# Loading an adjacency pair from two DMA queues: lower half on SyncE's, upper half on GpSimd's

## The chip, the cores and the metric

The kernel runs on one core of a Trainium2 chip, and its time is the device time of that core in microseconds. TensorE multiplies, VectorE transposes and does two-input arithmetic, ScalarE evaluates Ln, Exp and Square, GpSimd does a little arithmetic and issues DMAs, and SyncE only issues DMAs. In the profile they are called PE, DVE, ACT, POOL and SP. The 16 DMA engines are shared. A DMA issued by SP shows as q1 (hardware queue) and one issued by POOL as q0 (software queue).

## The reference

Two graph layers over 4096 nodes with 128 features. All matrices are float32, and `adj` is dense with 64 MB.

```python
h = jnp.maximum(_layernorm(x), 0.0)
msg = h @ W0 + B
sens = jnp.exp(-(1.0 / adj - 1.0) ** 2 / (2.0 * 0.5 * 0.5))
x = x + jnp.where(adj < 1.0, sens, 0.0) @ msg            # layer 0

h = jnp.maximum(_layernorm(x), 0.0)
A_hat = adj + jnp.eye(4096)
d = jnp.sum(A_hat, axis=1) ** (-0.5)
x = x + jax.nn.relu((d[:, None] * A_hat * d[None, :]) @ (h @ W1.T))   # layer 1
```

Row block r of layer 1 needs `support` of all column blocks, and `support` of block c needs the finished layer 0 of rows c. So a block (r, c) with c < r can be multiplied at once, and the others are kept for later.

## The kernel before

The matrix is cut in 8 x 8 blocks of 512 x 512 (`G = 8`). A block with its eight row groups is a *unit* u (64 in all, eight per block row, row g holds units 8g to 8g+7), and two units side by side are a *pair* n (32 in all, four per row). A pair is 2 MB and is loaded into `raw[:, n % 2]`: 128 partitions with 16 pieces of 256 floats (1 KB) each. Four DMAs bring it, one per quadrant of 32 partitions (`for q in range(Q)`), 512 KB each. Quadrants 0 and 1 are partitions 0 to 63, the lower half here, and quadrants 2 and 3 are the upper half.

For each unit DVE transposes `raw` into `kept[:, u % 4]` (`turn`, line 648), then takes the entries below the cutoff into `wt[:, u % 6]` (`cut`, line 663). ACT makes the weights from `wt` in four passes (Ln, Exp, Square, Exp: lines 528, 533, 538, 547; for every odd unit of rows 0 to 2 DVE takes over the square, line 669, and ACT's last pass is line 544). PE multiplies `wt` with `msg` into `acc0` (line 377), three units behind DVE (`LAG`). The row sums for layer 1 come from PE in rows 0 to 2 (`sum_tiles`, line 407) and from DVE in rows 3 to 7 (`row_sum`, line 656, once per pair, which reads `raw` too).

A block that layer 1 can use at once is multiplied from `kept` (`mix_once`, line 390). The 35 others are written to memory as 1 MB tiles (`store`, line 291, SP) and loaded again (line 345, POOL) into one of three `late` slots, and at the end into `raw`, for `mix_late` (line 399). Which late tile is multiplied at which unit is written out in the table `JOBS`; 20 late tiles are used inside the loop over units (`IN_TURN`) and 15 behind it (`TAIL`). At the end of each row PE, ACT and DVE pass the finished layer 0 rows to and fro (`copy_x1t` 573, `turn_x1` 430, `make_x1` 745, `log_pows` 577, `copy_hid` 585, `make_support` 774).

Three orders matter here. **SP's queue** is one list: the weights, `x` and pairs 0 and 1, then for each unit u the `store(u)`, if it is kept for later, and after each odd u the four DMAs of pair u // 2 + 2. The load waits until both units of the pair that had the buffer are turned, and from row 3 on until its `row_sum` is done. **POOL's queue** holds four memsets, the identity, 24 `tensor_scalar` for layer 0's first norm (line 330, three groups that wait for DVE's moments) and then the late loads in the order in which they are used. Late load j waits for the multiplication that frees its slot (`late_done`) and for its store (`spilled`). **DVE** waits in `turn` for `raw_loaded` at each even unit. A semaphore counts 16 per DMA.

Of the kernel before, what the change touches and what calls it, by code (L numbers as in the profile page):

```python
# [19 lines left out]
C4 = 4  # L20
Q = 4
B = 32
# [13 lines left out]
def col(u):  # L36

    return ORDER[u // G][u % G]
# [49 lines left out]
    return sum(not squared_by_dve(v) for v in range(u + 1))  # L88

def first_job(u):

    return sum(len(JOBS[v]) for v in JOBS if v < u)
# [10 lines left out]
def slot_before(j):  # L104

    return max((i for i in range(j) if late_slot(i) == late_slot(j)), default=None)

def slot_count(j):
# [4 lines left out]
def build(nc, x, adj, w0, b0, w1, out):  # L114
# [6 lines left out]
    with ctx:  # L121
# [64 lines left out]
        x_loaded = [sem(f"x_loaded{i}") for i in range(C4)]  # L186
        w_loaded = sem("w_loaded")
        raw_loaded = [sem(f"raw_loaded{i}") for i in range(RAW)]
        spilled = [sem(f"spilled{i}") for i in range(KEPT)]
        late_loaded = [sem(f"late_loaded{i}") for i in range(LATE + 2 * RAW)]  # L190
        out_written = [sem(f"out_written{i}") for i in range(2)]
# [80 lines left out]
        @block.sync  # L272
        def _(sp):
            def load(n):
                g = n // C4
                if n >= RAW:
                    if n - RAW >= PE_SUMS * C4:
                        sp.wait_ge(summed, n - RAW + 1 - PE_SUMS * C4)
                    sp.wait_ge(turned, 2 * (n - RAW + 1))
                for q in range(Q):  # L280
                    sp.dma_start(raw[q * B:(q + 1) * B, n % RAW],  # L281
                                 adj_parts[g // 2, g % 2, col(2 * n) // 2, q]).then_inc(raw_loaded[n % RAW], 16)

            def load_x(c):
                for h in range(2):
                    for q in range(Q):
                        sp.dma_start(x1[q * B:(q + 1) * B, c * 8 + h * T:c * 8 + h * T + T],
                                     x_parts[c, h, q]).then_inc(x_loaded[c], 16)

            def store(u):  # L290
                sp.dma_start(spill[u // G, col(u)],
                             kept[:, u % KEPT].rearrange("p k i -> p (k i)")).then_inc(spilled[u % KEPT], 16)

            sp.dma_start(w0_sb[:], w0).then_inc(w_loaded, 16)
            sp.dma_start(w1_sb, w1).then_inc(w_loaded, 16)
            sp.dma_start(b_row, b0.rearrange("(a d) -> a d", a=1)).then_inc(w_loaded, 16)
            load_x(0)
            load(0)
            load_x(1)
            load(1)  # L300
            load_x(2)
            load_x(3)
            for u in range(UNITS):
                if spills(u):
                    sp.wait_ge(turned, u + 1)
                    store(u)
                if u % 2 == 1 and u // 2 + RAW < PAIRS:
                    load(u // 2 + RAW)
            for i, r in enumerate(ENDS):
                sp.wait_ge(out_done, i + 1)  # L310
                for q in range(Q):
                    sp.dma_start(out_parts[r // 2, r % 2, q],
                                 fin[i % 2][q * B:(q + 1) * B]).then_inc(out_written[i % 2], 16)
            for i in range(2):
                sp.wait_ge(out_written[i], 64 * (G // 2))

        @block.gpsimd
        def _(pool):
            nc.gpsimd.memset(ident[:], 0.0).then_inc(ident_zeroed, 1)
            nc.gpsimd.memset(ones_row, 1.0)  # L320
            nc.gpsimd.memset(ones[:], 1.0)
# [9 lines left out]
                                                   ALU.subtract, ALU.max)  # L331
                last.then_inc(h0_done, 1)

            for j, (r, c) in enumerate(LOADED):
                slot = late_slot(j)
                u = r * G + ORDER[r].index(c)
                before = slot_before(j)
                if before is not None:
                    pool.wait_ge(late_done, before + 1)
                elif slot >= LATE:  # L340
                    last_pair = PAIRS - RAW + (slot - LATE) // 2
                    pool.wait_ge(summed, last_pair + 1 - PE_SUMS * C4)
                    pool.wait_ge(turned, 2 * last_pair + 2)
                pool.wait_ge(spilled[u % KEPT], 16 * spill_count(u))
                pool.dma_start(late_tile(slot).rearrange("p k i -> p (k i)"),  # L345
                               spill[r, c]).then_inc(late_loaded[slot], 16)

        @block.tensor
        def _(pe):
# [285 lines left out]
        def _(dve):  # L635
            def turn(u):
                n, h = u // 2, col(u) % 2
                if u % 2 == 0:
                    dve.wait_ge(raw_loaded[n % RAW], 64 * (n // RAW + 1))
                if u >= KEPT:  # L640
                    v = u - KEPT
                    if spills(v):
                        dve.wait_ge(spilled[v % KEPT], 16 * spill_count(v))
                    if at_once(v):
                        dve.wait_ge(once_done, once_count(v))
                dst = kept[:, u % KEPT].rearrange("p k (e i) -> p e k i", i=B)
                src = raw[:, n % RAW].rearrange("p e (k h i) -> p e k h i", k=T, h=2)[:, :, :, h, :]
                nc.vector.transpose(dst, src).then_inc(turned, 1)  # L648
# [213 lines left out]
```

## Time and profile before

| | us |
|---|---|
| median of 3 runs | 627.53 (626.89 to 627.85) |
| the profiled execution | 632.89 |
| its span, first to last instruction | 631.1 |
| PE, DVE, ACT, POOL busy | 537.5, 485.1, 466.0, 39.6 |

All terms below are worked out on the span of the profiled execution. No engine is busy all the time, so the question for each row of blocks is which of them, or the DMA engines, has no slack there. The slices of the page show this over time, the chain of work shows what the end hangs on, and the windows by row give busy time against length.

### The profile page before, as it was taken

How to read it: one execution, taken by the hardware profiler on the slowest of the kernel's cores; microseconds unless marked ns; L12 is line 12 of the kernel's file. 1: busy time of each engine (PE TensorE's matmuls, PEld its weight loads, DVE VectorE, ACT ScalarE, POOL GpSimd, SP SyncE). 2: the span in 40 equal slices, each digit the busy share in tenths (PEclk: the TensorE clock that was granted, in tenths of full speed). 3: DMA queues.
4: the chain of work that ended last, by engine and by line, in shares of the span. 5: the costliest groups of instructions: out<-in, count | busy, mean ns of one | idle time of the engine just before them, and what ended most of it. 6: DMA issues, size and time to landing. Idle time of an engine off the chain costs nothing.

```text
span 631.1 us, 4420 instructions
## 1 busy us (share of the span) xinstructions
PE 537.5 (85%) x1509; PEld 243.6 (39%) x1509; DVE 485.1 (77%) x555; ACT 466.0 (74%) x306; POOL 39.6 (6%) x68
## 2 busy tenths in 40 slices
PE   2446896969877998779769999979999999999995
PEld 2133432323322443334324444434444444444442
DVE  2799977789759899989989979986799849202056
ACT  2286878789967969999999969992999777920010
POOL 0241500000000000000000000000000000101100
PEclk9997998879888999989979999979999999999998
DMA  7999999999999959999999999999699951295623
GB/s 151 197 277 272 277 335 278 277 265 245 313 300 265 202 102 303 307 233 188 306 304 201 203 212 282 270 266 197 236 224 219 233 126 67 93 376 226 236 60 75
DMA packets 87193, 145.14 MB, mean 230 GB/s; under 512 B 4225, under 2 KB 78210, under 8 KB 78210
## 3 DMA queue, kind: packets, MB, share of 16 engines
q1 hardware_dynamic: 82130, 108.15, 75.2%
q0 software_dynamic: 5040, 36.70, 16.2%
q8 instruction: 12, 0.20, 0.1%
q14 instruction: 11, 0.09, 0.0%
HBM read 106.04 MB, written 38.80 MB: 230 GB/s over the span
## 4 chain that ended last, share of the span: by engine, by line
PE 42%; DVE 21%; ACT 14%; DMA 12%; issue 7%; SPq 4%; DVEq 0%
PE acc L377 13%; DMA raw<-in_adj_dram 12%; PE mix L399 11%; PE mix L390 11%; DVE kept L648 9%; DVE wt L663 4%; ACT wt L528 3%; ACT wt L533 3%; ACT wt L538 3%; SPq L281 3%; ACT wt L547 3%; DVE wt L669 2%; DVE rowpart L656 2%; PE acc L399 2%; PE side L399 1%
## 5 line engine op out<-in xcount | busy, mean ns | idle before, releaser
L377 PE MATMUL acc<-wt,msg 128*128 128x512 f32 x512 | 242.0, 617 | 4.7 <-ACT wt L547 4.7
L648 DVE STREAM_TRANSPOSE kept<-raw 128x2048 f32<-128x2048 f32 x64 | 147.6, 2306 | 42.9 <-DMA raw<-in_adj_dram 31.4
L377 PEld LDWEIGHTS acc<-wt,msg 128*128 128x128 f32 x512 | 98.6, 199 | 134.1 <-issue 124.3
L528 ACT ACTIVATE wt<-wt 128x2048 f32<-128x2048 f32 x64 | 121.9, 1905 | 38.1 <-DVE wt L663 38.1
L663 DVE SCALAR_TENSOR_TENSOR wt<-kept 128x2048 f32<-128x2048 f32 x64 | 146.5, 2288 | 1.5
L533 ACT ACTIVATE wt<-wt 128x2048 f32<-128x2048 f32 x64 | 121.6, 1900 | 0.4
L390 PE MATMUL mix<-kept,support 128*128 128x512 f32 x224 | 106.2, 620 | 13.0 <-DVE kept L648 6.5
L547 ACT ACTIVATE wt<-wt 128x2048 f32<-128x2048 f32 x52 | 98.8, 1899 | 0.0
L538 ACT ACTIVATE wt<-wt 128x2048 f32<-128x2048 f32 x52 | 98.7, 1898 | 0.0
L399 PE MATMUL mix<-late,support 128*128 128x512 f32 x200 | 89.7, 592 | 0.0
L656 DVE TENSOR_REDUCE rowpart<-raw 128x16 f32<-128x4096 f32 x20 | 87.6, 4379 | 0.0
L390 PEld LDWEIGHTS mix<-kept,support 128*128 128x128 f32 x224 | 43.6, 199 | 69.9 <-issue 59.6
L407 PE MATMUL mix<-kept,ones 128*32 128x512 f32 x192 | 33.0, 768 | 32.0 <-DVE kept L648 32.0
L399 PEld LDWEIGHTS mix<-late,support 128*128 128x128 f32 x200 | 37.9, 190 | 47.4 <-issue 47.4
L345 POOL DMA_DIRECT2D late<-adj_t_spill x27 | 14.4, 535 | 489.8 <-PE mix L399 381.3
L745 DVE TENSOR_TENSOR x<-side,x 128x512 f32<-128x512 f32 x8 | 5.5, 688 | 45.2 <-PE side L430 45.2
L573 ACT COPY x1t<-acc 128x512 f32<-128x512 f32 x8 | 4.7, 581 | 47.3 <-PE acc L377 47.3
L669 DVE SCALAR_TENSOR_TENSOR wt<-wt 128x2048 f32<-128x2048 f32 x12 | 27.4, 2287 | 4.5 <-ACT wt L533 4.5
L632 ACT COPY kept<-mix 128x512 f32<-128x512 f32 x6 | 3.5, 586 | 29.9 <-PE mix L399 26.6
L330 POOL TENSOR_SCALAR support<-x,mv 128x128 f32<-128x128 f32 x24 | 20.1, 856 | 49.6 <-DVE mv L688 49.6
L544 ACT ACTIVATE wt<-wt 128x2048 f32<-128x2048 f32 x12 | 22.8, 1898 | 0.0
L407 PEld LDWEIGHTS mix<-kept,ones 128*32 128x32 f32 x192 | 4.1, 117 | 46.8 <-DVE kept L648 41.1
(87 smaller groups left out, 260.8 us busy)
## 6 DMA issues: line engine op xcount, KB each, us to landing
raw<-in_adj_dram SPq DMA_DIRECT2D x128, 512.0 KB, 12.5
adj_t_spill<-kept SPq DMA_DIRECT2D x35, 1024.0 KB, 13.4
late<-adj_t_spill POOLq DMA_DIRECT2D x27, 1024.0 KB, 10.9
raw<-adj_t_spill POOLq DMA_DIRECT2D x8, 1024.0 KB, 6.2
x<-in_x_dram SPq DMA_DIRECT2D x32, 64.0 KB, 7.5
out_dram<-kept SPq DMA_DIRECT2D x32, 64.0 KB, 1.8
w_sb<-in_L_gnn_W_dram SPq DMA_DIRECT2D x1, 64.0 KB
late<-in_L_gnn_W_dram SPq DMA_DIRECT2D x1, 64.0 KB
```

Source lines behind the costliest of these rows:

```text
L377: mm = nc.tensor.matmul(acc0[:], msg[:, col(u) * T + k, :], wt[:, u % WTS, k, :], start=(first and k == 0), stop=(last and k == T - 1))
L390: mm = nc.tensor.matmul(once_bank[g][:], support[:, c * T + k, :], kept[:, u % KEPT, k, :], start=(first and k == 0), stop=False)
L399: mm = nc.tensor.matmul(bank[:], support[:, c * T + k, :], late_tile(slot)[:, k, :], start=(start and k == 0), stop=(stop and k == T - 1))
L407: mm = nc.tensor.matmul(bank[k * B:(k + 1) * B, :], ones[:], kept[:, u % KEPT, k, :], start=(u % G == 0), stop=(u % G == G - 1))
L528: nc.scalar.activation(v, v, ACT.Ln, bias=LN_GUARD).then_inc(ln_done, 1)
L533: nc.scalar.activation(v, v, ACT.Exp, scale=-1.0).then_inc(inv_done, 1)
L538: nc.scalar.activation(v, v, ACT.Square, bias=-1.0).then_inc(square_done, 1)
L547: nc.scalar.activation(v, v, ACT.Exp, scale=-2.0).then_inc(wt_done, 1)
L648: nc.vector.transpose(dst, src).then_inc(turned, 1)
L656: nc.vector.tensor_reduce(dst, src, AX_X, ALU.add).then_inc(summed, 1)
L663: nc.vector.scalar_tensor_tensor(out=wt[:, u % WTS], in0=v, scalar=CUTOFF, in1=v, op0=ALU.is_lt, op1=ALU.mult).then_inc(cut_done, 1)
L669: nc.vector.scalar_tensor_tensor(out=v, in0=v, scalar=-2.0, in1=v, op0=ALU.add, op1=ALU.mult).then_inc(quad_done, 1)
```

## The change

Each pair n with n < 2 or n >= 4 (30 of the 32) is loaded from two queues: SP issues quadrants 0 and 1, POOL quadrants 2 and 3, each with a semaphore of its own (`raw_loaded`, `upper_loaded`). Pairs 2 and 3 stay with SP as a whole. POOL's waits before its half are the same as SP's (`turned`, `summed`). DVE's wait before the transposition of an even unit becomes two waits. POOL issues the halves of pairs 0 and 1 before its memsets, and those of pairs 4 to 31 behind the 24 `tensor_scalar`. The 20 late loads of `IN_TURN`, which stood in a row behind each other before, now stand among the upper halves: late load j behind the half of pair `load_pair(j)`, which is 8 + j or three pairs behind the unit whose multiplication frees the slot, whichever is later. That gives pairs 8, 9, 10, 11, 15, 17, 19, 20, 22, 23, 24, 25, 26, 27, 27, 28, 29, 30, 31, 31 for j = 0 to 19. No bytes and no arithmetic are added or taken away.

```diff
+UPPER_FIRST = C4
+LOADED_FIRST = 2 * C4
+
+def upper_on_pool(n):
+    return n < RAW or n >= UPPER_FIRST
+
+def load_pair(j):
+    before = slot_before(j)
+    if before is None:
+        return LOADED_FIRST + j
+    return max(LOADED_FIRST + j, first_unit(before) // 2 + RAW + 1)
...
-                for q in range(Q):
+                for q in range(Q // 2 if upper_on_pool(n) else Q):
                     sp.dma_start(raw[q * B:(q + 1) * B, n % RAW],
                                  adj_parts[g // 2, g % 2, col(2 * n) // 2, q]).then_inc(raw_loaded[n % RAW], 16)
...
+            def load_upper(n):
+                g = n // C4
+                if n >= RAW:
+                    if n - RAW >= PE_SUMS * C4:
+                        pool.wait_ge(summed, n - RAW + 1 - PE_SUMS * C4)
+                    pool.wait_ge(turned, 2 * (n - RAW + 1))
+                for q in range(Q // 2, Q):
+                    pool.dma_start(raw[q * B:(q + 1) * B, n % RAW],
+                                   adj_parts[g // 2, g % 2, col(2 * n) // 2, q]).then_inc(upper_loaded[n % RAW], 16)
+
+            for n in range(RAW):
+                load_upper(n)
...
+            for n in range(UPPER_FIRST, PAIRS):
+                load_upper(n)
+                for j in range(len(IN_TURN)):
+                    if load_pair(j) == n:
+                        load_late(j)
+            for j in range(len(LOADED)):
+                if j >= len(IN_TURN) or load_pair(j) >= PAIRS:
+                    load_late(j)
...
-                    dve.wait_ge(raw_loaded[n % RAW], 64 * (n // RAW + 1))
+                    dve.wait_ge(raw_loaded[n % RAW], lower_count(n))
+                    dve.wait_ge(upper_loaded[n % RAW], upper_count(n))
```

POOL before, from its start. `late` in line 320 is the row of ones, and line 330 makes layer 0's normalized rows; the rows from line 345 on are the late loads.

```order
L319 MEMSET ident 128x128
L320 MEMSET late 1x128
L321 MEMSET ones 128x32
L322 MEMSET thirty_second 128x1
L324 ISA
L324 AFFINE_SELECT ident<-ident 128x128
L330 TENSOR_SCALAR support<-x,mv 128x128 x24
L345 DMA late<-adj_t_spill 128x2048 x23
```

POOL after, the same stretch. Line 361 is an upper half (two DMAs per pair), line 393 a late load.

```order
L361 DMA raw<-in_adj_dram 32x16x256 x4
L366 MEMSET ident 128x128
L367 MEMSET late 1x128
L368 MEMSET ones 128x32
L369 MEMSET thirty_second 128x1
L371 ISA
L371 AFFINE_SELECT ident<-ident 128x128
L377 TENSOR_SCALAR support<-x,mv 128x128 x24
L361 DMA raw<-in_adj_dram 32x16x256 x10
L393 DMA late<-adj_t_spill 128x2048
L361 DMA raw<-in_adj_dram 32x16x256 x2
L393 DMA late<-adj_t_spill 128x2048
```

Four DMAs moved ahead of the memsets, and the first late load moved behind ten DMAs (pairs 4 to 8).

SP before, from its start through the loads of pairs 2 to 4. Line 287 loads `x`, line 281 pairs, and line 291 is a store.

```order
L287 DMA x<-in_x_dram 32x4x128 x8
L281 DMA raw<-in_adj_dram 32x16x256 x4
L287 DMA x<-in_x_dram 32x4x128 x8
L281 DMA raw<-in_adj_dram 32x16x256 x4
L287 DMA x<-in_x_dram 32x4x128 x16
L291 DMA adj_t_spill<-kept 128x2048 x2
L281 DMA raw<-in_adj_dram 32x16x256 x4
L291 DMA adj_t_spill<-kept 128x2048 x2
L281 DMA raw<-in_adj_dram 32x16x256 x4
L291 DMA adj_t_spill<-kept 128x2048 x2
L281 DMA raw<-in_adj_dram 32x16x256 x4
```

SP after, the same stretch, where the same operations are lines 322, 316 and 326.

```order
L322 DMA x<-in_x_dram 32x4x128 x8
L316 DMA raw<-in_adj_dram 32x16x256 x2
L322 DMA x<-in_x_dram 32x4x128 x8
L316 DMA raw<-in_adj_dram 32x16x256 x2
L322 DMA x<-in_x_dram 32x4x128 x16
L326 DMA adj_t_spill<-kept 128x2048 x2
L316 DMA raw<-in_adj_dram 32x16x256 x4
L326 DMA adj_t_spill<-kept 128x2048 x2
L316 DMA raw<-in_adj_dram 32x16x256 x4
L326 DMA adj_t_spill<-kept 128x2048 x2
L316 DMA raw<-in_adj_dram 32x16x256 x2
```

Only the number of DMAs per load has changed. Each load still stands behind two stores, and the other two DMAs of the pair stand behind none.

## Rows read from the trace of the kernel before

**Rows 1.** Windows, one per block row (rows 0 to 6).

```profile
core 0: us, PE busy (x) PEld busy (x) DVE busy (x) ACT busy (x) POOL busy (x), PEclk, DMA share, GB/s
19.68:89.02 69.34, 43.55 (x174) 22.13 (x175) 64.04 (x135) 52.38 (x39) 21.32 (x26) 0.90 1.10 269
89.02:150.32 61.30, 47.08 (x154) 18.10 (x153) 50.08 (x45) 48.12 (x31) 0.00 (x0) 0.86 1.07 279
150.32:215.10 64.78, 55.34 (x174) 21.81 (x173) 50.07 (x46) 54.09 (x35) 1.06 (x2) 0.89 1.06 271
215.10:278.11 63.01, 53.81 (x137) 24.24 (x136) 60.03 (x47) 57.15 (x37) 1.06 (x2) 0.97 0.95 233
278.11:338.78 60.67, 51.00 (x126) 22.92 (x125) 58.10 (x46) 59.22 (x38) 1.05 (x2) 0.94 1.08 256
338.78:401.45 62.67, 62.67 (x160) 28.69 (x159) 58.03 (x47) 55.85 (x35) 2.11 (x4) 1.00 1.01 238
401.45:472.00 70.55, 66.60 (x163) 30.11 (x162) 58.10 (x48) 59.36 (x38) 2.64 (x5) 0.95 0.96 232
```

**Rows 2.** The chain that ended last: start us, us, what.

```profile
69.78 19.21 DMA raw<-in_adj_dram
...
305.71 17.53 DMA raw<-in_adj_dram
...
325.62 6.15 PE mix L390 x8
```

**Rows 3.** Timeline of DVE: start, us, then [idle before <-releaser].

```profile
19.68 2.31 DVE L648 STREAM_TRANSPOSE kept<-raw 128x2048 f32<-128x2048 f32 x1 [8.41 <-DMA raw<-in_adj_dram]
...
77.78 2.30 DVE L648 STREAM_TRANSPOSE kept<-raw 128x2048 f32<-128x2048 f32 x1
...
89.02 2.31 DVE L648 STREAM_TRANSPOSE kept<-raw 128x2048 f32<-128x2048 f32 x1 [4.54 <-DMA raw<-in_adj_dram]
...
417.76 2.31 DVE L648 STREAM_TRANSPOSE kept<-raw 128x2048 f32<-128x2048 f32 x1 [2.96 <-DMA raw<-in_adj_dram]
...
448.10 2.30 DVE L648 STREAM_TRANSPOSE kept<-raw 128x2048 f32<-128x2048 f32 x1
```

**Rows 4.** Windows of single kinds of traffic (columns as in rows 1).

```profile
205.00:216.00 11.00, 11.00 (x38) 5.12 (x37) 9.47 (x13) 10.97 (x7) 0.00 (x0) 1.00 1.10 200
212.00:212.50 0.50, 0.50 (x9) 0.38 (x8) 0.46 (x3) 0.50 (x1) 0.00 (x0) 1.00 0.96 231
...
217.00:217.50 0.50, 0.50 (x3) 0.25 (x2) 0.41 (x1) 0.50 (x1) 0.00 (x0) 1.00 1.08 264
...
36.00:40.00 4.00, 0.44 (x3) 0.04 (x1) 3.96 (x3) 3.97 (x6) 0.00 (x0) 1.00 1.00 411
558.00:562.00 4.00, 4.00 (x11) 1.79 (x10) 0.00 (x0) 0.00 (x0) 0.53 (x1) 1.00 1.01 426
```

**Rows 5.** Waits of ACT in block rows 1 and 2: us, times, longest.

```profile
ACT x1t L573 <- PE acc L377: 4.4, 1, 4.4
...
ACT x1t L573 <- PE acc L377: 4.3, 1, 4.3
```

**Rows 6.** Timeline of POOL: start us, us, then [idle before <-releaser].

```profile
1.22 0.28 POOL L324 TENSOR_SCALAR_AFFINE_SELECT ident<-ident 128x128 f32<-128x128 f32 x1
...
63.91 7.30 POOL L330 TENSOR_SCALAR support<-x,mv 128x128 f32<-128x128 f32 x8 [14.99 <-DVE mv L688]
...
434.64 0.53 POOL L345 DMA_DIRECT2D late<-adj_t_spill  x1 [20.19 <-PE mix L399]
```

**Rows 7.** Timeline of PE at the start.

```profile
11.41 1.94 PE L355 MATMUL mix<-ident,support 128*128 128x128 f32 x8 [6.89 <-DVE support L695]
```

**Rows 8.** Late loads, line 345: duration min/median/max, then issue to landing.

```profile
L345 POOL DMA_DIRECT2D late<-adj_t_spill x27: 527/527/718, 71.2 to 592.5; - x27
...
DMA to landing us min/median/max: 5.0/10.4/14.5
```

**Rows 9.** A wait on DVE's sequencer.

```profile
L645 DVEq EVENT_SEMAPHORE  x11: 21/21/21, 224.9 to 518.7; - x11
```

More of the change, by code:

```diff
@@ L88, in act_squares, with upper_count, lower_count @@
     return sum(not squared_by_dve(v) for v in range(u + 1))
+UPPER_FIRST = C4
+LOADED_FIRST = 2 * C4
+def upper_on_pool(n):
+    return n < RAW or n >= UPPER_FIRST
+def upper_count(n):
+    return sum(32 for m in range(n % RAW, n + 1, RAW) if upper_on_pool(m))
+def lower_count(n):
+    return sum(32 if upper_on_pool(m) else 64 for m in range(n % RAW, n + 1, RAW))
 def first_job(u):
@@ L106, in slot_before, with first_unit @@
     return max((i for i in range(j) if late_slot(i) == late_slot(j)), default=None)
+def load_pair(j):
[3 more added lines that the diff above has]
+    return max(LOADED_FIRST + j, first_unit(before) // 2 + RAW + 1)
+def first_unit(j):
+    return [u for u in sorted(JOBS) for _ in JOBS[u]][j]
 def slot_count(j):
@@ L188, in build @@
         raw_loaded = [sem(f"raw_loaded{i}") for i in range(RAW)]
+        upper_loaded = [sem(f"upper_loaded{i}") for i in range(RAW)]
         spilled = [sem(f"spilled{i}") for i in range(KEPT)]
@@ L332, in _, with load_late @@
                 last.then_inc(h0_done, 1)
-            for j, (r, c) in enumerate(LOADED):
+            def load_late(j):
+                r, c = LOADED[j]
                 slot = late_slot(j)
```

## The prediction

> **What bounds the kernel now.** I read the windows first, cut at the transposition that opens each block row [rows 1]. Compare the length of a window with the busy time of each engine in it. From 338.8 on PE fills its rows (62.67 of 62.67 us in block row 5). From 215 to 339 DVE (60.0 of 63.0) and ACT (59.2 of 60.7) are nearly full. But in block rows 1 and 2 (89.0 to 215.1) nobody is: of 61.3 and 64.8 us the busiest engine has 50.1 and 55.3, and PE's figure is inflated, since its granted clock was 0.86 and 0.89 there, a mixture of stretches at 2.4 and at 1.2 GHz. The last column names the one without slack: the DMA share is 1.06 to 1.10. The chain of waits says the same. It runs through loads of `raw` before 323 us, 19.2 us of it in one piece before unit 8, and behind the load that ends at 323 it goes over into PE's work [rows 2]. So only the first 323 us have something to give. What is gained there should reach the end, since what follows is PE's and ACT's work, in the same order.
>
> **Why the DMA engines are full.** They move 200 GB/s while only pairs are loaded, 411 while stores are written, and 426 while late tiles are read [rows 4]. Stores and late tiles span 128 partitions, a pair's DMA spans 32. One reason could be the 1 KB pieces, the other the partitions. The trace decides between them: in the long run of pair loads around 205 to 223 there are short peaks, 231 GB/s at 212.0 and 264 at 217.0 [rows 4]. They are 5 us apart, which at 200 GB/s is two quadrants (1.05 MB / 200 GB/s = 5.2 us). At every second change of quadrant, then, while some engines are still in one half of the partitions and others already in the other, the same 1 KB pieces go 1.3 times as fast. So each half of the partitions has a limit of its own near 200 GB/s, and a loader that works in one half at a time gets one half's rate. Two queues, one per half, can keep that peak up.
>
> The Trainium skill (SBUF — State Buffer, "Door 1: the DMA port swizzle") says that partitions 0 to 63 reach 8 of 16 ports; that would cap a quadrant's DMA at half the rate, and the trace agrees (200 against 426 GB/s). The Trainium skill's section "Can I just issue two DMAs to hit both halves?" on the same page speaks against the change, though: two concurrent DMAs on the two halves measured only 6% over one. By that figure a pair would take 9.9 us, an estimate from that page, where the row below takes 7.9. The peak of 264 against 200 is more than 6%, but it lasts half a microsecond. That case is the first rival.
>
> **What DMA work costs per row.** One pair alone takes 2.10 MB / 200 GB/s = 10.5 us, a store 1.05 MB / 411 = 2.55, a late tile 1.05 / 426 = 2.46. Block row 1 has 4 pairs and 7 stores: 41.9 + 17.9 = 59.8 of the 61.3 us that it lasts, which confirms that the row is the DMA engines'. With both halves at once I take 264 GB/s, so 7.9 us a pair, and block row 1 needs 31.8 + 17.9 = 49.7. The end values for a pair are 10.5 (no gain) and 5.0 (both halves at the 426 of a 128-partition read).
>
> **Start.** The first transposition waits 8.4 us for pair 0 and begins at 19.7 [rows 3]. Its upper half now starts at once, beside `x` and the lower half. The data to move before unit 0 (0.5 MB of `x`, pair 0, and about as much of pair 1 that now competes) is some 3.6 MB, at 264 GB/s 13.6 us after the first issue, so unit 0 begins near 16. **-4**, with 0 and -7 as ends. The four issues ahead of the memsets cost 4 x 0.53 = 2.1 us if a 512-piece DMA costs POOL what a 128-piece one does [rows 8], and 8.4 if four times that. The identity, done at 1.5 [rows 6], is then ready at 3.6 to 9.9. PE first needs it in earnest at 11.4, when DVE's rows are there [rows 7], so this is free. Without that cover it would be the 2.1 to 8.4 us.
>
> **Block row 0** is DVE's: 64.0 of 69.3 us busy [rows 1], and 4.5 of the rest is one wait for pair 4 at 89.0 [rows 3]. That wait should go, since two late loads (4.9 us of traffic) leave this stretch for pairs 8 and 9, and pair 4's upper half no longer stands behind two stores. But POOL can issue it only behind the last `tensor_scalar` group, which ends at 71.2 now [rows 6], some 4 us behind the time at which the buffer is free. **-4.5**, ends 0 and -5.
>
> **Block rows 1 and 2** last 126.1 us. Without the DMA limit ACT is next: 48.1 + 54.1 = 102.2 us busy [rows 1]. It does not get there, because at each change of row ACT stands for `acc0` (4.4 and 4.3 us [rows 5]) and for the short chain behind it, which are no waits for loads. I add 5 us per row: 112. Row 2 also gets four late loads where it had two: 31.8 + 6 x 2.55 + 4 x 2.46 = 56.9 us of DMA work, so it sits at both limits; 1 us more. 113, **-13**, ends -2 (DMA work at 10.5 a pair) and -20.
>
> **Block rows 3 and 4.** Row 3 goes from 63.0 to about 61 (DVE busy 60.0), row 4 from 60.7 to about 60.2 (ACT busy 59.2) [rows 1]. **-2.5**. **Rows 5 to 7 and the tail** are PE's; I take **-1** of the 3.0 us for which unit 50 waits for its pair [rows 3], since PE has a backlog there.
>
> **What is added.** 60 DMAs leave SP for POOL: 60 x 0.53 = 32 us of POOL's time, up to 127 if a 512-piece DMA costs four times as much. POOL is busy for 39.6 of 631 us, and per pair it has 13 us or more for 1.1 to 4.2. DVE's second wait costs 30 x 0.021 = 0.6 us at the row of such a wait [rows 9], inside the roundings above. POOL's queue is in order, so a late load that waits for PE holds the upper halves behind it. The longest-lagging one is j = 14, now at 434.6 [rows 6]; the half of pair 28 behind it needs unit 53's transposition, which starts at 448.1 [rows 3]. So it holds up nothing, with 13 us to spare.
>
> Sum: -4 - 4.5 - 13 - 2.5 - 1 = **-25**. The span of 631.1 becomes 606.1, the profiled time of 632.9 becomes 607.9. Taking the same 25 off the median of 627.5 gives **602.5 us**. Ends: with every term at its better value (-7, -5, -20, -3.5, -3) about 589; with a mixed rate just above 200, see the first rival.
>
> **Rival 1, the halves do not add up.** Both queues use the same engines, and the peak may only be engines that happen to be out of step. Then a pair still takes 10.5 us. Left are the better start (-3), the late loads out of row 0 (-4.5, with 2 to 5 back in row 2), 1.5 in row 1 and 2 in row 3: about -8, so 619 (624 with the start's gain lost and 5 back in row 2). With a quarter of the peak's gain, 0.65 us a pair over the 12 pairs of rows 0 to 2, it is 612. (By the 6% of the Trainium skill, SBUF — State Buffer, "Can I just issue two DMAs to hit both halves?", it would be about 612 too, an estimate from that page.) For it: the recorded peaks stay under 270 where 400 would be possible. Against it: they come at every change of half.
>
> **Rival 2, slower: POOL cannot write the pieces fast enough.** A late load is 128 pieces, an upper quadrant 512. The trace has no 512-piece DMA from POOL. The 0.53 us of its record may not be the whole price: from issue to landing a late tile takes at least 5.0 us [rows 8], of which 2.5 is transfer. If the other 2.5 were all piece-writing, a quadrant would take 10 us and a pair 20, four pairs 80 us against rows of 61 to 65: every row is POOL's then, and the kernel takes 700. It decides from about 15 us per pair, the 61 us of a row over four. In the case just beyond, 17 us a pair, 8 rows of 68 instead of 65 make it 650. Against it: POOL's own record of a late load is 0.53 us in the median and 0.72 at most over 27 of them [rows 8], which four times over is 2.1 a quadrant and 4.2 a pair. That row is nearest, so I keep the case small.
>
> **Rival 3, late tiles come too late.** They now stand behind upper halves in POOL's queue, and the halves share their ring. A late tile lands 10.4 us after issue in the median [rows 8] and is used 2 to 4 units (14 us and more) behind its new place. If landing went to 18 us, PE would lose about 4 us at five places: 20 of the 25 us, so 623; at six places and more, nothing is left.
>
> **Chances.** As forecast (594 to 611) 0.67; rival 1 0.17; rival 2 0.09; rival 3 0.07. Range 594 to 620: it holds the forecast's own ends but for the very best, more than half of rival 1 and some of rival 3, and leaves rival 2 out. A measurement of this kernel can tell 0.2% (1.3 us) from no change. Faster by more than that: the forecast, rival 1 and most of rival 3, 0.87; within it 0.04; slower 0.09.
>
> **What would show it.** Right: in windows without stores, pair loads move clearly over 200 GB/s; the load pieces of the chain before 323 us shrink; unit 8 opens near 80 and block row 3 near 194; rows 1 and 2 show ACT near 9 tenths; the last 290 us look as before, only earlier. Rival 1: 200 GB/s stays, DMA share over 1.05 in rows 1 and 2. Rival 2: POOL's DMA records of 2 us and more, the upper semaphore last in every wait of DVE. Rival 3: PE waits for `late` at line 399 of before. I would be wrong altogether if row 1, without DMA waits, still took 60 us, because PE's half-clock stretches, not loads, set its pace.

## The result, and the profile after

The changed kernel takes **624.44 us** (median of 5 runs, 622.34 to 625.09) against 627.68 for the kernel before beside it: a ratio of 0.9935, 95% interval 0.9908 to 0.9962. A second set (after_again) gave 623.85 (8 runs) against 629.71, 0.9917 (0.9884 to 0.9949). It is faster by 3 to 6 us, where I had forecast 25, and the forecast range ended at 620.

Both kernels were profiled twice, and the profiles can be cut at the same transpositions as in [rows 1]. All numbers are us; the start is the time at which unit 0 opens, "rest" runs from unit 40 to the end of the span.

| | start | row 0 | rows 1+2 | rows 3+4 | rest | span |
|---|---|---|---|---|---|---|
| before, as in [rows 1] | 19.7 | 69.3 | 126.1 | 123.7 | 292.3 | 631.1 |
| before, second profile | 19.3 | 70.0 | 127.0 | 122.8 | 288.0 | 627.0 |
| after | 22.7 | 64.7 | 124.0 | 120.5 | 288.3 | 620.2 |
| after, second profile | 22.8 | 64.7 | 125.1 | 120.3 | 288.8 | 621.7 |
| forecast, against the first line | -4 | -4.5 | -13 | -2.5 | -1 | -25 |

So the first 339 us scatter by about 1 us from one profile of a kernel to the next, and the rest by 4. Of the 10.9 us between the first two profiles, the 4.0 in the rest are scatter of one profile of before. What the change really moved is +3 at the start, -5 in row 0, about -2 in rows 1 and 2, and -3 in rows 3 and 4.

The windows after, of block rows 0 to 2, are these (columns as in rows 1):

```profile
core 0: us, PE busy (x) PEld busy (x) DVE busy (x) ACT busy (x) POOL busy (x), PEclk, DMA share, GB/s
22.72:87.44 64.72, 43.03 (x179) 23.63 (x178) 63.96 (x134) 48.84 (x38) 22.78 (x28) 0.79 1.06 256
87.44:150.13 62.69, 50.99 (x174) 19.80 (x173) 50.16 (x47) 53.94 (x35) 6.35 (x10) 0.89 0.98 270
150.13:211.46 61.33, 51.61 (x173) 20.45 (x172) 50.08 (x46) 52.68 (x34) 6.38 (x10) 0.94 1.06 306
```

Row 0 is now full of VectorE's work (63.96 of 64.72). Rows 1 and 2 are still full of nobody's: 50.2 and 50.1 us of DVE, 53.9 and 52.7 of ACT, in windows of 62.7 and 61.3.

**The start went the wrong way.** The timeline of DVE at the start:

```profile
17.33 1.64 DVE L742 BATCH_NORM_STATS2 bn<-x 128x6 f32<-128x128 f32 x8 [17.33 <-DMA x<-in_x_dram]
...
22.72 2.31 DVE L706 STREAM_TRANSPOSE kept<-raw 128x2048 f32<-128x2048 f32 x1 [1.30 <-DMA raw<-in_adj_dram]
```

DVE now waits for `x`, not for pair 0: it has `x` at 17.33, and had it at 7.18 before. The queues (name, kind: packets, MB, share of 16 engines) show why, first between 3 and 8 us, then between 8 and 16:

```profile
q0 software_dynamic: 256, 0.98, 85.0%
q1 hardware_dynamic: 223, 0.11, 12.7%
...
q0 software_dynamic: 311, 1.08, 70.5%
q1 hardware_dynamic: 1012, 0.51, 37.6%
```

**The loads of a pair, later on.** The two queues between 104 and 106 us, while the halves of one pair are under way and a store (issued at 96.5) is as good as done:

```profile
DMA packets 207, 0.52 MB, mean 258 GB/s; under 512 B 9, under 2 KB 108, under 8 KB 205
...
q0 software_dynamic: 104, 0.40, 80.6%
q1 hardware_dynamic: 103, 0.12, 26.6%
```

Together they move 258 GB/s, near the 264 that I had read from a peak. But the two queues send one packet for one (104 and 103), so the upper half gets 0.40 of the 0.52 MB. The upper half is soon done, and the lower one runs on by itself. With loads alone the same holds over 20 us (bench_queues below, 70 to 90 us):

```profile
q0 software_dynamic: 1143, 4.16, 79.0%
q1 hardware_dynamic: 1144, 1.14, 26.1%
```

The pair costs its mean, not its peak. The Trainium skill (DMA: Bandwidth & Descriptors, "Queues, rings and completion order") says that each DMA engine goes round the queues packet by packet; by that rule packet sizes set the shares, and this trace agrees, with 104 packets against 103.

**The waits of DVE in rows 1 and 2** (us in all, times, longest). First before, 89 to 215, then after, 87.4 to 211.5:

```profile
DVE kept L648 <- DMA raw<-in_adj_dram: 13.2, 4, 4.5
DVE kept L648 <- issue: 11.5, 2, 7.6
...
DVE wt L669 <- ACT wt L533: 3.8, 3, 2.1
```

```profile
DVE wt L727 <- ACT wt L590: 10.0, 4, 6.4
...
DVE kept L706 <- issue: 7.6, 2, 6.4
DVE kept L706 <- DMA raw<-in_adj_dram: 5.1, 5, 2.5
```

The two waits at the transposition (the profile names no releaser for part of them) fell from 24.7 to 12.7 us, which is the size of the -13 forecast. The wait for ACT's pass rose from 3.8 to 10.0. Here is where it arises, unit 10 of row 1, in the timelines of ACT, PE and DVE:

```profile
106.07 0.56 ACT L612 COPY hid_t<-mix 128x512 f32<-128x512 f32 x1
...
115.67 0.59 ACT L630 COPY x1t<-acc 128x512 f32<-128x512 f32 x1 [5.27 <-PE acc L434]
```

```profile
106.69 1.57 PE L471 MATMUL side<-thirty_second,hid_t 128*128 128x1 f32 x8 [4.48 <-ACT hid_t L612]
...
110.05 5.58 PE L434 MATMUL acc<-wt,msg 128*128 128x512 f32 x8
...
123.50 2.29 DVE L727 SCALAR_TENSOR_TENSOR wt<-wt 128x2048 f32<-128x2048 f32 x1 [6.40 <-ACT wt L590]
```

PE's order at the third unit of a row has `turn_sums` (line 471) ahead of the row's last `multiply_weights`. So PE waits 4.48 us for ACT's `hid_t`, which stands in ACT's queue behind the passes of an earlier unit. Behind that wait PE runs at a granted clock of 0.51, its level of 1.2 GHz, as this window shows (columns as in rows 1):

```profile
107.00:110.00 3.00, 3.00 (x15) 1.37 (x14) 2.97 (x2) 2.97 (x2) 0.79 (x2) 0.51 1.13 203
```

The row's last product takes 5.58 us where the next one, at 117.05, takes 3.60. ACT needs that product for `x1t` and waits 5.27; DVE needs ACT's pass behind `x1t` and waits 6.40. This ring (PE for ACT, ACT for PE, DVE for ACT) holds no wait for a load.

ACT's waits in rows 1 and 2 of before, 89 to 215, add up to what the rows lasted:

```profile
ACT x1t L573 <- PE acc L377: 8.7, 2, 4.4
ACT wt L528 <- DVE wt L663: 7.8, 5, 3.7
ACT inv L577 <- DVE pows L763: 5.0, 2, 3.3
ACT hid_t L585 <- PE side L436: 2.1, 2, 1.3
```

With 102.2 us of work that is 125.8 of 126.1 us. At most the 7.8 us behind DVE's `cut` are the loads'; 15.8 us are hand-overs at the change of row. These rows were in the trace when the forecast was made.

**POOL writes the pieces easily.** Its record of the 60 upper quadrants (min/median/max, ns) and their time from issue to landing:

```profile
L361 POOL DMA_DIRECT2D raw<-in_adj_dram x60: 652/652/807, 1.3 to 486.5; - x60
...
DMA to landing us min/median/max: 5.7/10.5/14.5
```

A DMA of 512 pieces costs POOL 0.65 us where one of 128 costs 0.53 [rows 8].

### The profile page after: what moved, and what is told of

Same layout as the page of the kernel before. It is cut to its first block, busy times and chain, and to the rows that moved or that the text cites. A ratio compares the mean times of both kernels' runs of the same rounds, so it can differ in the third digit from the quotient of the medians.

```text
span 620.2 us, 4442 instructions
## 1 busy us (share of the span) xinstructions
PE 531.5 (86%) x1509; PEld 241.4 (39%) x1509; DVE 484.9 (78%) x555; ACT 465.8 (75%) x306; POOL 79.9 (13%) x128
## 4 chain that ended last, share of the span: by engine, by line
PE 41%; DVE 24%; ACT 13%; DMA 10%; issue 9%; POOL 1%; SPq 1%; DVEq 0%
PE acc L434 14%; PE mix L456 12%; PE mix L447 10%; DMA raw<-in_adj_dram 10%; DVE kept L706 9%; DVE wt L721 5%; ACT wt L585 3%; ACT wt L590 3%; ACT wt L595 3%; ACT wt L604 3%; DVE rowpart L714 2%; DVE wt L727 2%; PE acc L456 2%; POOL support L377 1%; PE side L456 1%
## 5 line engine op out<-in xcount | busy, mean ns | idle before, releaser
L434 PE MATMUL acc<-wt,msg 128*128 128x512 f32 x512 | 244.5, 623 | 4.7 <-ACT wt L604 4.7
L447 PE MATMUL mix<-kept,support 128*128 128x512 f32 x224 | 102.4, 602 | 5.6 <-ACT mixed L646 4.7
L361 POOL DMA_DIRECT2D raw<-in_adj_dram x60 | 39.4, 662 | 361.3 <-DVE rowpart L714 229.2
L464 PE MATMUL mix<-kept,ones 128*32 128x512 f32 x192 | 30.0, 701 | 21.9 <-DVE kept L706 21.9
L727 DVE SCALAR_TENSOR_TENSOR wt<-wt 128x2048 f32<-128x2048 f32 x12 | 27.5, 2288 | 10.9 <-ACT wt L590 10.9
L601 ACT ACTIVATE wt<-wt 128x2048 f32<-128x2048 f32 x12 | 22.8, 1899 | 0.0
```

Source lines behind the costliest of these rows:

```text
L361: pool.dma_start(raw[q * B:(q + 1) * B, n % RAW], adj_parts[g // 2, g % 2, col(2 * n) // 2, q]).then_inc(upper_loaded[n % RAW], 16)
L434: mm = nc.tensor.matmul(acc0[:], msg[:, col(u) * T + k, :], wt[:, u % WTS, k, :], start=(first and k == 0), stop=(last and k == T - 1))
L447: mm = nc.tensor.matmul(once_bank[g][:], support[:, c * T + k, :], kept[:, u % KEPT, k, :], start=(first and k == 0), stop=False)
L727: nc.vector.scalar_tensor_tensor(out=v, in0=v, scalar=-2.0, in1=v, op0=ALU.add, op1=ALU.mult).then_inc(quad_done, 1)
```

## The experiments

Rates, starts and waits are from one profile of each kernel, times are medians of 4 to 10 runs (2 for `sums_later_quarter`). The table gathers what the cuts of each profile give.

| kernel | start | row 0 | rows 1+2 | rows 3+4 | rest | ratio to before (95%) |
|---|---|---|---|---|---|---|
| start_on_sp | 19.0 | 66.1 | 124.1 | 121.1 | 287.7 | 0.9874 (0.9844 to 0.9904) |
| x_first | 21.5 | 65.4 | 125.3 | 121.9 | 287.9 | 0.989 (0.9825 to 0.9955) |
| late_order_only | 19.0 | 64.9 | 132.8 | 124.9 | 287.5 | 1.0031 (1.0008 to 1.0054) |
| quarter_loads | 19.2 | 64.7 | 123.0 | 120.4 | 289.3 | 0.9799 (0.9763 to 0.9834) |
| sums_later | 19.5 | 69.5 | 124.8 | 124.5 | 292.2 | 1.0028 (0.9987 to 1.0068) |
| order_and_later | 19.8 | 64.7 | 132.5 | 125.1 | 288.4 | 1.0053 (1.0028 to 1.0079) |
| sums_later_quarter | 19.3 | 64.7 | 111.8 | 120.4 | 290.3 | 0.9683 (0.9584 to 0.9782) |
| sums_later_split | 19.5 | 65.8 | 118.4 | 120.1 | 288.9 | 0.9808 (0.9726 to 0.9889) |
| x_first_later | 21.2 | 65.2 | 119.6 | 120.9 | 288.3 | 0.98 (0.9746 to 0.9854) |
| split_on_act | 21.4 | 72.2 | 120.2 | 122.4 | 290.6 | 1.0037 (1.0006 to 1.0069) |
| act_order_later | 19.4 | 64.7 | 119.3 | 125.6 | 292.5 | 0.9932 (0.9903 to 0.996) |

**The loads alone, in five ways (bench_queues).** It computes nothing and writes zeros: six pairs per stage, each stage behind the end of the one before.

> Loads only, no arithmetic (the output is zeros). Five stages, each loads 6 pairs (12.6 MB) into buffers of their own and waits for all: (0) one queue, quadrant after quadrant, as before; (1) lower halves on SP's queue, upper halves on POOL's, as in the change; (2) lower halves on SP's queue, upper on ACT's (a second hardware queue); (3) one queue, DMAs of 16 partitions, halves in turn; (4) one queue, quadrants in the order 0, 2, 1, 3. Theory A (the halves add up, but POOL's queue moves the pieces in packets of 4 KB and SP's in 1 KB, and the engines serve the queues packet by packet, so the upper half takes about four fifths of the time until it is done): stage 0 takes 63 us at 200 GB/s; stage 1 starts at about 250 GB/s with the upper half at 200 and the lower at 50, for 31 us, then 24 us of lower half alone at 195, together 55 us; stage 2, with equal packets, is even and reaches 264 GB/s or more, 48 us or less; stage 3 between 231 and 264 GB/s, 48 to 55 us; stage 4 has a change of half per quadrant, 58 to 60 us. Theory B (the engines give no more in two queues than in one, what the change gained is queue order): all five stages 60 to 63 us.

Windows: one queue; SP and POOL over the whole stage, in its first part and in its last part; SP and ACT; DMAs of 16 partitions.

```profile
core 0: us, POOL busy (x), PEclk, DMA share, GB/s
5.00:60.00 55.00, 0.00 (x0) 1.00 1.13 211
62.50:117.00 54.50, 7.82 (x12) 1.00 1.03 231
70.00:80.00 10.00, 0.58 (x1) 1.00 1.05 264
100.00:110.00 10.00, 0.00 (x0) 1.00 1.13 205
120.00:150.00 30.00, 0.00 (x0) 1.00 1.07 334
...
180.00:200.00 20.00, 0.00 (x0) 1.00 1.15 114
```

SP and POOL move 264 GB/s only while both have work. POOL's half ends first, SP finishes alone at 205, and the stage as a whole runs at 231: 9.1 us per pair of 2.10 MB, against 9.9 at 211. Two hardware queues move 334. Here the packets are equal (1 KB), and each queue moved 5.01 MB of the 10.01 in that window. From first issue to last landing the five stages took 61.7, 54.5, 40.7, 112.7 and 59.5 us for 12.58 MB each: theory A, but for the fourth. The Trainium skill (SBUF — State Buffer, "Can I just issue two DMAs to hit both halves?") gives 6% for two concurrent DMAs on the two halves. Here SP and POOL gain 13% (61.7 against 54.5 us) and SP and ACT 52% (61.7 against 40.7), so the measurement decides. DMAs of 16 partitions (114) were a miss of mine: I had expected 231 to 264. The fifth stage, quadrants in the order 0, 2, 1, 3 from one queue, came as expected (59.5 us, 58 to 60 forecast): more changes of half are worth 2 us in six pairs.

**The first two pairs from SP again (start_on_sp).**

```diff
-    return n < RAW or n >= UPPER_FIRST
+    return n >= UPPER_FIRST
...
-            for n in range(RAW):
-                load_upper(n)
```

> The changed kernel with pairs 0 and 1 loaded by SP alone again; pairs 4 to 31 stay split. Theory A (packets of 4 KB of two pairs in POOL's queue hold up the 512-byte packets of x): DVE has x at about 7 us instead of 17.3, the first transposition opens at 19.7 instead of 22.7, and the 3 us reach the end: 621 us, 0.990 of before. Rival (DVE's work in block row 0 and the late tensor_scalar group of POOL set the pace, not the start): the first transposition is 3 us earlier, but the end moves by less than 1 us, 624.

621.54 us. Its DVE has `x` back at 7.19 and starts where the kernel before did:

```profile
7.19 1.64 DVE L741 BATCH_NORM_STATS2 bn<-x 128x6 f32<-128x128 f32 x8 [7.19 <-DMA x<-in_x_dram]
...
19.04 2.31 DVE L705 STREAM_TRANSPOSE kept<-raw 128x2048 f32<-128x2048 f32 x1 [7.76 <-DMA raw<-in_adj_dram]
```

So the lost start was `x` behind POOL's large packets. Row 0 gives 1.4 of the 3.7 us back, since DVE catches up there.

**The first pairs from POOL, but behind x (x_first).** In the changed kernel, `load_upper(0)` and `load_upper(1)` stand behind `x_loaded[0]` and `x_loaded[1]`.

> Only the start differs from the changed kernel: GpSimd still issues the upper halves of pairs 0 and 1, but each behind the landing of the x rows of its group, so that its large packets no longer run beside the small ones of x. Theory A (x was starved by the upper halves, and both queues together are faster than one): VectorE has x at about 7 us, the upper half of pair 0 and its lower half then run beside each other, unit 0 opens at 17 to 18.5 us, earlier than the 19.7 of the kernel before and the 19.0 of the variant whose first pairs are all SP's; the time is 4 us under the changed kernel, 620. Theory B (two queues at the start gain nothing once x is served first, since the upper half now begins later): unit 0 opens at 20 to 22 us and the time is 622 to 624.

623.75 us, and unit 0 opens at 21.5: theory B. DVE has `x` at 7.31, but pair 0 comes later than from SP alone, 19.0. Between 14 and 21.5 the DMA engines move only 189 to 210 GB/s. So two queues buy nothing at the start, even with `x` served. The two halves of pair 0 hardly run beside each other: all 838 packets between 8 and 12 us are SP's, although POOL issued at 7.6 and 8.4, and SP's half has landed by 14.6. What runs beside POOL's half afterwards is the next group of `x`. Why POOL's packets begin so late I did not find out.

**The late loads' order alone (late_order_only).** All of `adj` from SP, the late loads in the places of the change.

> All pairs on SP's queue as before, but POOL issues the late loads at the places of the change (behind the same waits as its halves had). Theory A (the split brings the gain, the order is only what it needs): within 2 us of before, 626 to 629 us. Theory B (the gain is queue order: two late loads leave block row 0): unit 8 opens 3 to 5 us earlier than the 89.0 of before, and the time is that of the change, 623 to 625 us.

631.58 us. Row 0 takes 64.9 us without any split. So the -4.6 of row 0 belongs to the order, which takes two late loads out of it. Rows 1 and 2 take them back, with 132.8 in place of 126 to 127, and so the time met neither theory.

**A quarter of each pair (quarter_loads).** The kernel before, but from pair 2 on only 4 of 16 pieces are loaded; the other 12 keep what the buffer held.

```diff
-                    sp.dma_start(raw[q * B:(q + 1) * B, n % RAW],
+                    e = 16 if n < RAW else 4
+                    sp.dma_start(raw[q * B:(q + 1) * B, n % RAW, 0:e],
...
```

> The kernel before, in which pairs 2 to 31 bring only 4 of 16 row pieces (a quarter of the bytes; the rest of the buffer is stale, so the output is not the reference's), so that loads limit nothing. The theory of the prediction (without the limit of the loads rows 1 and 2 take 113 us together, as ACT's 102 us of work plus 10): block rows 1 and 2 take 110 to 114 us, rows 3 and 4 120, time 598 to 604 us. Rival (hand-overs between PE, ACT and DVE and PE's stretches at 1.2 GHz fill the rows, so loads were not all of the limit): rows 1 and 2 take 118 to 124 us, time 612 to 620 us.

617.14 us. This is the run that decided. The DMA share in rows 1 and 2 is about half, DVE no longer waits for `raw`, and yet the two rows take 123.0 us:

```profile
83.90:145.57 61.67, 48.75 (x167) 19.25 (x160) 49.98 (x47) 52.54 (x34) 0.53 (x1) 0.86 0.55 179
145.57:206.87 61.30, 53.09 (x173) 21.05 (x172) 49.98 (x46) 52.81 (x34) 0.53 (x1) 0.89 0.47 154
```

```profile
120.32 2.29 DVE L670 SCALAR_TENSOR_TENSOR wt<-wt 128x2048 f32<-128x2048 f32 x1 [7.88 <-ACT wt L534]
...
181.62 2.29 DVE L670 SCALAR_TENSOR_TENSOR wt<-wt 128x2048 f32<-128x2048 f32 x1 [7.51 <-ACT wt L534]
```

Where DVE does not wait for loads it waits for ACT, 7.88 and 7.51 us, in the same place of each row as above. ACT's own waits (83.9 to 206.9) are these:

```profile
ACT x1t L574 <- PE acc L378: 10.9, 2, 5.6
ACT inv L578 <- DVE pows L764: 3.5, 2, 1.7
ACT hid_t L586 <- PE side L437: 2.7, 2, 1.3
```

With the 105.4 us of work in the windows above that is 122.5 of the 123.0 us. With PE's order as it stood, no way of loading could bring rows 1 and 2 to 113. What they had to give was 3 to 4 us, and of that the change took 2.

**Opening the ring.** PE's order at the third unit is turned round, so that the row's last product comes first:

```diff
-                if 1 <= g <= PE_SUMS and idx == 2:
-                    turn_sums(g - 1)
...
                     multiply_weights(u - LAG)
+                if 1 <= g <= PE_SUMS and idx == 2:
+                    turn_sums(g - 1)
```

This was put into the kernel before (sums_later), into start_on_sp (sums_later_split), and into quarter_loads (sums_later_quarter, which leaves out the same pieces of `adj`).

> The same move of turn_sums in the kernel before, all pairs on SP. Theory C with loads as a second limit just behind the hand-over: rows 1 and 2 cannot fall under their DMA work of 59.8 and 62.2 us, so 0 to 5 us are gained, 624 to 630 us. If the hand-over alone was the limit: 620 us or less. Theory D: 629 to 631 us.

> start_on_sp (split from pair 4 on), and PE's small multiplication of the row sums (turn_sums) stands behind multiply_weights in its unit instead of ahead of it; nothing else moves. Theory C (what fills block rows 1 to 3 besides loads is a hand-over in a ring: PE waits in turn_sums for ACT's copy_sums, then multiplies the last weights of the row, ACT stands 5 us for that in copy_x1t, DVE stands 6 us for ACT): ACT's wait for acc at copy_x1t in rows 1 to 3 falls from 4 to 5 us to under 2, block rows 1 and 2 take 4 to 8 us less than the 124 of start_on_sp, time 611 to 617 us. Theory D (the rows are full because of PE's stretches at 1.2 GHz and the order makes no difference): 620 to 623 us.

> The same move with a quarter of each pair's bytes from pair 2 on (stale rest, so the output is not the reference's). Theory C: with loads out of the way the whole of the hand-over shows, block rows 1 and 2 fall from 123 us to 112 to 117, time 604 to 611 us. Theory D: 616 to 618 us, rows 1 and 2 at 123.

631.58, **616.09** and 609.21 us. Rows 1 and 2 of the second, and what has become of PE's wait in it:

```profile
85.31:142.66 57.35, 49.38 (x165) 19.80 (x164) 50.09 (x46) 53.94 (x35) 6.35 (x10) 0.91 1.05 295
142.66:203.72 61.06, 51.15 (x172) 20.18 (x171) 49.98 (x46) 53.46 (x34) 6.37 (x10) 0.94 1.06 306
```

```profile
104.57 1.05 PE L469 MATMUL side<-thirty_second,hid_t 128*128 128x1 f32 x8 [0.82 <-ACT hid_t L610]
```

PE waits 0.82 us in place of 4.48. The two limits cover each other: with the ring alone gone, 1 to 2 us in rows 1 and 2 and nothing in the time (sums_later, 1.6 us above the range of theory C); with the load limit alone lifted, 3 to 4 us in rows 1 and 2 (quarter_loads); with both lifted, 14 to 15 (111.8). The forecast's 113 is near what the rows take with neither limit.

**Both edits around the split, without it (order_and_later).** late_order_only with the move of `turn_sums`.

> The kernel before with the late loads in the order of the change and with turn_sums moved behind multiply_weights, but all loads of adj from SyncE alone. Theory A (in block rows 1 and 2 loads at one queue's rate are a limit of their own, and only the split lifts it): rows 1 and 2 take 125 to 128 us as before, and the time is 628 to 631, no difference that can be told. Theory B (what the best variant gained came from order and move together, the split added its own only in block row 0): rows 1 and 2 take 119 to 121 us, and the time is 620 to 623. By the DMA work at 10.5 us a pair row 1 has 4 pairs, 7 stores and little else, 60 us, and row 2 67 us with four late loads, so 127 in all: I expect A.

631.80 us, and rows 1 and 2 take 132.5. DVE's wait at the transposition over the whole kernel is the longest of all:

```profile
L700 DVE STREAM_TRANSPOSE kept<-raw 128x2048 f32<-128x2048 f32 x64 | 147.6, 2306 | 50.6 <-DMA raw<-in_adj_dram 36.9 <-issue 13.6
```

So in sums_later_split the split itself is what gives: 132.5 against 118.4, 14 us in rows 1 and 2, or 1.8 us per pair over their 8 pairs.

**The upper half on ScalarE's queue (split_on_act, act_order_later).** ACT issues the upper halves, in 1 KB packets like SP's. The first has the late loads in their old order and ACT's DMAs behind its Ln. The second is order_and_later with the split from pair 4 on, and the DMAs ahead of the Ln up to row 2.

> The kernel before with the upper halves of pairs 0, 1 and 4 to 31 on ACT's hardware queue (behind the Ln of the odd unit two pairs ahead, where its waits are met), POOL's late loads in their old order, pair 0's upper half behind the first x. In the loads-only run two hardware queues gave 347 GB/s, POOL's 264. Theory A and C together (loads stop to be a limit, hand-overs remain): the first transposition at 14 to 16 us instead of 19, rows 1 and 2 near the 123 us of quarter loads, time 613 to 619 us, faster than start_on_sp. Against it: ACT is 98% busy in block row 4, and each issue takes its sequencer 0.5 us and more, 30 us in all; if that stands in ACT's way the time is 630 us or more.

> As the run before, but the upper half of each pair from pair 4 on is issued by ScalarE on a hardware queue of its own, with pieces and packets of 1 KB like SyncE's, in front of its Ln of the odd unit (behind it from block row 3 on). Theory A (the unequal packets, 4 KB on GpSimd's queue and 1 KB on SyncE's, cost the split kernel its rate, and the earlier run on ScalarE failed by the order of its late loads): pairs arrive sooner than with GpSimd, VectorE hardly waits for raw, rows 1 and 2 take 112 to 116 us, 118.4 with GpSimd, and the time is 610 to 614, 0.971 to 0.977 of the kernel before. Theory B (small packets of both halves lose against the 8 KB packets of stores and late loads, so that a pair is late whenever one of these runs beside it): VectorE waits 15 us or more for raw in all, rows 1 and 2 take 118 or more, and the time is 617 to 625.

630.92 and 624.22 us, although this pair of queues was by far the fastest when loads were alone. The first is a miss: 613 to 619 was expected. Its row 0 takes 72.2 us, and unit 8 waits for pair 4 until 93.6. The queues between 82 and 86 us, while two late loads (q0) and a store (q1) run beside ACT's half of pair 4 (q10), show why:

```profile
q0 software_dynamic: 112, 0.79, 46.9%
q1 hardware_dynamic: 109, 0.79, 46.7%
q10 hardware_dynamic: 112, 0.11, 7.7%
```

Again it is one packet for one, now among three queues, and with packets of 1 KB beside two queues of 8 KB ACT's half gets 0.11 of 1.7 MB. So a pair is late beside large packets, as theory B of act_order_later has it. In act_order_later between 126 and 132 us, while both halves of pair 8 are under way with a late load, it is not so plain:

```profile
q1 hardware_dynamic: 621, 0.66, 51.2%
q0 software_dynamic: 98, 0.80, 44.8%
q10 hardware_dynamic: 55, 0.06, 2.9%
```

ACT's half again gets little (q10), and pair 8, issued at 122.7 and 124.8, lands at 146.9. But of the 668 packets under 2 KB in that window some 580 are SP's lower half, also in 1 KB packets beside the same late load. So packet size alone does not explain this window, and its cause stays open.

Nor does it explain why the kernel with ACT ends 8 us behind the one with POOL (624.22 against 616.09). Rows 1 and 2 take 119.2 us, hardly more than 118.4, and DVE's wait at the transposition over the whole kernel is 22.7 us against 24.8. 5.5 of the 8 us lie in rows 3 and 4 (125.6 against 120.1), and the 292.5 of the rest is within the scatter seen for before. What lengthens rows 3 and 4 was not tried. Theory B's time and rows came true (617 to 625, 118 or more), its reason only in part.

**Both improvements (x_first_later).**

> The variant before with one more edit, turn_sums of the previous row moved behind multiply_weights in PE's order at the third unit of a row. Theory A (the hand-over at the row's start is PE's and ACT's, and the loads are the second limit, as the earlier runs with this move showed): rows 1 and 2 take 118 us in place of 124, the time is about 5 us under the variant without the move, 614 to 616, 0.977 to 0.980 of the kernel before, as good as the best so far or 1 to 2 us better by its start. Theory B (the gain of the move came from the first pairs' loads being SP's): rows 1 and 2 stay at 122 or more and the time at 619 or more.

617.73 us, 6 under x_first, which was timed in the same set, and rows 1 and 2 at 119.6: theory A for the move, though 2 us above its range. The start brings nothing: the two best kernels, this one (0.98) and sums_later_split (0.9808), cannot be told apart.

**The same kernels again (after_again, before_again).**

> The changed kernel as it stands, once more, so that it is timed and profiled beside the two variants below on one chip. Expected: 624 us, 0.993 of the kernel before; unit 0 opens near 22.7 us, unit 8 near 87.4, unit 24 near 211.5, and from unit 40 to the end 288 us pass. What differs in this profile from the first one is the scatter of one profile, and no difference between kernels smaller than it is to be read from single profiles.

> The kernel before as it stands, profiled a second time. Its first profile (632.9 us) lay 5 us above the median of its first three runs and 3 above that of the later ones, so part of the 11 us between the two first profiles belongs to this one profile. Theory A (the excess is scatter in block rows 1 and 2, where loads, stores and the hand-over at the row's start meet): this profile gives about 629, the blocks rows 1 and 2 take 122 to 124 us in place of 126.1, and block row 0 is 69 again. Theory B (the excess is spread over the whole span): all block rows are shorter by half a microsecond or so, and the gain of the changed kernel in block row 0 of 4.6 shrinks too. In both, unit 0 opens at 19 to 20.

after_again is as expected in every row but for 1 us. For before_again both theories fell. It took 628.89 us, rows 1 and 2 took 127.0 and not 122 to 124, and the excess of the first profile lay in the rest, 292.3 against 288.0.

## Why the prediction was wrong

**What bounds the kernel.** The reading that nobody is full, the DMA share is over 1 and so the DMA engines have no slack was half of it. The loads were a limit in rows 1 and 2, but a second one stood 3 us behind. The step that failed is the term "-13": "I add 5 us per row: 112". Both of its parts were too small. The 5 us came from ACT's waits of 4.4 and 4.3 for `acc0` [rows 5], taken as they stood while loads were slow, and left 0.65 us a row for "the short chain behind it", which in the same trace cost 7.1 us in the two rows (5.0 and 2.1, above). When loads do not hold DVE (quarter_loads), ACT waits 10.9 us for `acc0` and 6.2 us in the chain, so 8.5 a row and not 5. And ACT's work is 105.4 us and not 102.2: the window of row 1 in [rows 1] holds only 31 of ACT's operations, where those of quarter_loads hold 34 each. That gives the 123.0. The measured rows of the changed kernel, 124.0, have 106.6 us of ACT's work, 9.0 for `acc0`, 6.3 in the chain and 1.8 behind DVE's `cut`. The text named this case last, as what would make it wrong altogether ("PE's half-clock stretches, not loads"), and gave it no price and no chance. The experiments show the order on PE as its cause, by moving one operation. That 113 lies near the 111.8 of sums_later_quarter is luck: there the work is 105.2 us and the waits 6.5, since the wait for `acc0` is gone.

**The rate of a pair.** 264 GB/s was right as a peak (258 in the window above, 264 with loads alone) and wrong as a mean: 231 GB/s, 9.1 us and not 7.9. Unequal packets let one half finish early. The rate alone would have cost part of the -13 even without the ring: 118.4 us (sums_later_split) against 111.8 with light loads, though these two also differ in the late loads' order. Rival 1 (halves that do not add up, 612 to 624) gives about the right time, for a reason that is only partly right.

**Start.** Forecast -4, measured +3. The step that put 0.5 MB of `x`, pair 0 and about as much of pair 1 at 264 GB/s added bytes and took the sharing as harmless. But `x` is what DVE needs first, it goes in the smallest packets, and it landed at 17.33 in place of 7.18. Neither end of my range (0 and -7) was a loss; the bound should have reached above zero, since traffic was put beside `x`.

**Block row 0.** Forecast -4.5, measured -4.6. Its reason, the late loads leaving, is shown by late_order_only; the split is not needed for it. **Rows 3 and 4** were forecast at -2.5 and measured at -3.2 (-2.5 between the second profiles). **The rest**: -1 forecast, 0 measured when second profiles are taken in too.

**What is added.** It held: POOL 0.65 us per quadrant, the identity ready at 4.8, and late loads that hold up nothing. Rival 2 is refuted by POOL's records, and rival 3 by PE's waits, none of which names a load of `late`. The price of moving late loads between rows was put at "2 to 5 back in row 2", and measured with SP's loads alone at 6 (132.8 against 127.0).

Together, against the second profile of before: +3.4 - 5.2 - 3.0 - 2.3 + 0.3 = -6.8 (627.0 to 620.2), and the medians say 3 to 6. Of the signs that I had named, unit 8 opens at 87.4 and not near 80, and block row 3 at 211.5 and not near 194.

## What to carry to other kernels

When a stretch has no full engine, a saturated resource is one limit and perhaps not the only one: before a gain of many us is put on relieving it, follow the hand-overs in it (who waits for whom at the row's start) and ask how long they would last if the resource were free. Loading only a quarter of each pair answers that in one run, and adding an engine's own waits to its work (here ACT's) answers most of it from the trace at hand. Here it would have capped the forecast at 13 us (617.14 against 630.17). And where two queues share the DMA engines, compare packet sizes first: a transfer in small packets, above all a short one that something waits for, can be starved beside large ones.

## What the hardware showed that I had not expected

- The same 1 KB pieces go as 4 KB packets from POOL's queue and as 1 KB packets from SP's and ACT's. While both run, packets are served one for one (1143 to 1144 with loads alone), so bytes go 3.6 to 1. In some stretches of the full kernels the counts are not equal (98 to 55 in act_order_later).
- One queue of 32-partition DMAs moves 211 GB/s, one of 16-partition DMAs 114, and two hardware queues, one per half of the partitions, 334 over 30 us.
- Of this fast pair of queues little is left to one half beside two queues of 8 KB packets: 0.11 MB in 4 us, of 1.7 MB in all (split_on_act).
- The time of a profile scatters in stretches where no edit was made, 4 us of 290, so a row that an edit does not touch belongs to the comparison.
